# Two row sums of a graph network's last node pass as adding DMAs instead of VectorE additions

## The reference

```python
h = jnp.maximum(_layernorm(x, axis=-1), 0.0)
x = x + _L0_gnn_ref(h, ..., src, dst)               # conv with attention, batch norm over all nodes
h = jnp.maximum(_layernorm(x, axis=-1), 0.0)
x = x + _L1_gnn_ref(h, edge_attr_32, edge_index_t, ...)

# inside _L1_gnn_ref
pairs = jnp.concatenate([node_vectors, boxes], axis=1)
c = _gelu(pairs @ W_c1 + b_c1)
combined = _gelu(c @ W_c2 + b_c2)
return node_vectors + combined
```

## Time and profile before

| what | value |
|---|---|
| median of 3 runs | 2105.99 us (2104.59 to 2109.98) |
| span of the profiled execution, first to last instruction | 1817.9 us |
| median of the runs less that span | 288.1 us |
| busy over the span: PE, PEld, DVE, ACT, POOL | 80%, 54%, 82%, 47%, 62% |
| mean granted TensorE clock | 0.851 of full speed |
| share of the 16 DMA engines: SP's queue, POOL's queue | 41.1%, 7.4% |
| DVE's first addition of the second node pass (L879) | at 743.2 us |
| its last row sum (L891) | at 1282.5 us |

### The profile page before, as it was taken

How to read it: one execution, slowest core, us unless ns; L and a number is a source line. 1 busy time by engine, 2 the same in 40 slices (tenths; PEclk the granted TensorE clock), 3 DMA queues, 4 the chain that set the end, 5 groups by cost and what they waited for, 6 DMA issues and landing times.

```text
span 1817.9 us, 22722 instructions
## 1 busy us (share of the span) xinstructions
PE 1463.3 (80%) x6619; PEld 980.4 (54%) x6619; DVE 1485.5 (82%) x2772; ACT 849.3 (47%) x1497; POOL 1129.4 (62%) x989
## 2 busy tenths in 40 slices
PE   3465556488888888588988988889599999999993
PEld 2133233367777777366656666666345555555541
DVE  8799999688988887798899789888268788788781
ACT  4477777322233222365666566665123433434341
POOL 7777788777777777787500000868756776434446
PEclk9788897667777777797899689888789999999996
DMA  7467664777754333344444434555344453343410
GB/s 232 156 219 229 210 212 157 245 249 261 269 200 130 120 108 110 120 169 159 153 151 165 143 142 163 179 181 174 115 114 146 129 150 106 112 129 101 123 52 17
DMA packets 139616, 286.41 MB, mean 158 GB/s; under 512 B 31154, under 2 KB 48379, under 8 KB 139496
## 3 DMA queue, kind: packets, MB, share of 16 engines
q1 hardware_dynamic: 107176, 254.36, 41.1%
q0 software_dynamic: 32320, 30.62, 7.4%
HBM read 164.51 MB, written 121.80 MB: 157 GB/s over the span
## 4 chain that ended last, share of the span: by engine, by line
PE 48%; DVE 29%; issue 11%; POOL 4%; ACT 4%; DMA 3%; SPq 0%; DVEq 0%; POOLq 0%; ACTq 0%
PE banks L1400 7%; DVE stat L697 5%; PE banks L1390 5%; PE banks L1454 4%; DVE stat L705 4%; PE banks L1321 3%; PE banks L1477 3%; PE banks L1475 3%; PE banks L1484 2%; DVE sums L780 2%; PE banks L1304 2%; DVE xc L711 2%; PE banks L1448 2%; POOL agg_ring L577 2%; PE banks L1372 2%
## 5 line engine op out<-in xcount | busy, mean ns | idle before, releaser
L577 POOL DMA_INDIRECT agg_ring<-agg_rows,edge_idx x196 | 234.6, 1197 | 331.4 <-DMA edge_agg<-agg_ring 270.1
L581 POOL DMA_INDIRECT out<-agg,put_last x196 | 207.6, 1059 | 167.1 <-DVE agg L976 109.9
L577 POOL DMA_INDIRECT x_ring<-in_x,edge_idx x200 | 239.8, 1199 | 63.3 <-issue 60.9
L581 POOL DMA_INDIRECT agg_rows<-agg,put_first x196 | 229.2, 1169 | 59.7 <-issue 57.9
L577 POOL DMA_INDIRECT gout<-in_x,edge_idx x192 | 217.1, 1130 | 58.5 <-issue 57.3
L1400 PEld LDWEIGHTS banks<-packed,cT 96*128 96x128 f32 (+1 forms) x1568 | 202.4, 207 | 43.3 <-issue 42.0
L1400 PE MATMUL banks<-packed,cT 96*128 96x64 f32 (+1 forms) x1568 | 208.8, 291 | 0.0
L1265 PE MATMUL banks<-ident,xc 128*128 128x128 f32 (+1 forms) x784 | 131.4, 316 | 94.1 <-DVE xc L711 94.1
L1265 PEld LDWEIGHTS banks<-ident,xc 128*128 128x128 f32 (+1 forms) x784 | 110.5, 165 | 147.1 <-DVE xc L711 107.7
L1274 PE MATMUL banks<-hT,packed 128*128 128x512 f32 (+1 forms) x196 | 126.8, 781 | 76.3 <-ACT hT L1031 76.3
L1390 PE MATMUL banks<-hT,packed 64*96 64x512 f32 (+1 forms) x392 | 128.5, 735 | 46.4 <-ACT cT L1131 40.8
(11 more groups left out here) (153 smaller groups left out, 3135.9 us busy)
## 6 DMA issues: line engine op xcount, KB each, us to landing
xt<-in_x SPq DMA_DIRECT2D x96, 512.0 KB, 4.2
r_rows<-rT SPq DMA_DIRECT2D x48, 512.0 KB, 5.9
xe<-edge_x SPq DMA_DIRECT2D x96, 256.0 KB, 4.6
agg_rows<-rb SPq DMA_DIRECT2D x48, 512.0 KB
rT<-r_rows SPq DMA_DIRECT2D x48, 512.0 KB, 5.6
out<-xt SPq DMA_DIRECT2D x48, 512.0 KB, 2.6
edge_r<-rr SPq DMA_DIRECT2D x48, 256.0 KB, 3.9
rr<-edge_r SPq DMA_DIRECT2D x48, 256.0 KB, 4.8
```

The source lines that it names most:

```text
L577: A.indirect_dma_start(to, None, table[:, :], bass.IndirectOffsetOnAxis(ap=idx, axis=0), bounds_check=limit, oob_is_err=False).then_inc(si ...
L581: A.indirect_dma_start(table[:, :], bass.IndirectOffsetOnAxis(ap=idx, axis=0), rows_of, None, bounds_check=limit, oob_is_err=False).then_i ...
```

## The change

The two DVE additions `add_h2` and `final_rows` of the second node pass become DMAs from SBUF to SBUF with an adding write, issued by POOL. Semaphores that counted DVE instructions become sets of DMA semaphores (`B_y` one of 3, `B_fin` one of 6). POOL's program is merged: `put_agg` of the first 36 groups (`PUTS_AHEAD`), then 51 turns, one for each step s: `add_h2(s)`, `add_out(s - 2)` and one group of agg's DMAs, `put_agg` of the groups 36 to 48 in turns 0 to 12 and `gather_agg(s - 13)` from turn 13 on; then the other 11 groups of `gather_agg`. SP stashes up to `a - 14` groups instead of `3 * (i - 16)`. The semaphores of the x loads of the second pass are those of the first pass, counted on.

```diff
+PUTS_AHEAD = 36
+FIN_LAG = 2
...
-    def __init__(self, sems, incs=16):
-        self.sems, self.incs = sems, incs
+    def __init__(self, sems, incs=16, first=0):
+        self.sems, self.incs, self.first = sems, incs, first
...
-        B_x = slots("rows_loaded", XS)
+        B_x = Slots(A_x.sems, first=S)
-        B_y = stage("x2_plus_h2")
+        B_y = slots("h2_added_to_x2", CS)
-        B_fin = stage("final_row_ready")
+        B_fin = slots("out_gelu_added", XS)
...
             def store_final(s):
-                sp.wait_ge(B_fin.sem, B_fin.after(s))
+                sp.wait_ge(B_fin.of(s), B_fin.after(s))
...
-                due = min(G, max(stashed, 3 * (i - 16)))
+                due = min(G, max(stashed, a - 1 - G + PUTS_AHEAD))
...
+            def add_h2(s):
+                p = nodes_of(s)
+                pool.wait_ge(B_h.sem, B_h.after(s))
+                A.dma_start(xt[s % XS][0:p, :], xc[s % CS][0:p, :], accum_op=ALU.add).then_inc(B_y.of(s), 16)
+
+            def add_out(s):
+                p = nodes_of(s)
+                pool.wait_ge(B_og.sem, B_og.after(s))
+                pool.wait_ge(B_y.of(s), B_y.after(s))
+                A.dma_start(xt[s % XS][0:p, :], gout[s % 2][0:p, :], accum_op=ALU.add).then_inc(B_fin.of(s), 16)
...
-            for n in range(G):
+            for n in range(PUTS_AHEAD):
                 put_agg(n)
-            G_p.all_done(pool, G)
-            for g in range(G):
+            for s in range(S + FIN_LAG):
+                if is_step(s):
+                    add_h2(s)
+                if is_step(s - FIN_LAG):
+                    add_out(s - FIN_LAG)
+                n = PUTS_AHEAD + s
+                if is_group(n):
+                    put_agg(n)
+                if n == G:
+                    G_p.all_done(pool, G)
+                if is_group(n - G):
+                    gather_agg(n - G)
+            for g in range(S + FIN_LAG + PUTS_AHEAD - G, G):
                 gather_agg(g)
...
-            def final_rows(s):
-            def add_h2(s):
...
-            for i in range(PAIRS + 1):
+            for i in range(PAIRS):
...
-                if is_step(a - 2):
-                    final_rows(a - 2)
...
-                if a in pair:
-                    add_h2(a)
-                if is_step(a - 1):
-                    final_rows(a - 1)
-                if b in pair:
-                    add_h2(b)
```

More of the change, by code:

```diff
@@ L55 @@
 class Slots:
-    def __init__(self, sems, incs=16):
-        self.sems, self.incs = sems, incs
+    def __init__(self, sems, incs=16, first=0):
+        self.sems, self.incs, self.first = sems, incs, first
     def of(self, step):
-        return self.sems[step % len(self.sems)]
+        return self.sems[(self.first + step) % len(self.sems)]
     def after(self, step):
-        return (step // len(self.sems) + 1) * self.incs
+        return ((self.first + step) // len(self.sems) + 1) * self.incs
     def done(self, eng, step):
@@ L506, in load_prev @@
                     sp.wait_ge(B_t.sem, B_t.after(S - 1))
-                    sp.wait_ge(B_y.sem, B_y.after(S - 1))
+                    B_y.all_done(sp, S)
                 load_same(mask[g % MS], prev_row, g, g, 0, P, C_sm)
```

## The result

The changed kernel took 2220.1 us (median of 4 runs, 2207.0 to 2227.1), the kernel before beside it 2108.0: +112 us. The ratio on record is 1.0633, 95% interval 1.0535 to 1.0731; that of the two medians is 1.053, and why the two differ is open. Forecast were +56 us and 2162; the sign and the range (2100 to 2245) held, the size was off by a factor of two.

The account below looks back on a forecast made before the run. PE's round, not DVE, was taken to bound the second pass. Pairs +49, start +18 and end -11 gave +56 on 2106, so 2162 us (range 2100 to 2245); 288 us outside the profiled span were taken as they are.

Parts of the forecast that it names:

- The old loop, -0.3 us a pair: Second node pass: removing four DVE additions a pair saves only 0.3 us, giving 20.3 us at full clock.
- d = 1.5: POOL's time to issue one SBUF-to-SBUF adding DMA, in us; high end 2.3, low end 1.27.
- c = 5.5: POOL's time for a group of four scatters, in us, range 5.1 to 5.9.
- L = 5.5: Time from issue to landing of an adding DMA, in us, range 3.4 to 9.
- POOL's work in a pair is then 17 us of about 21: Second pass: two groups and four adding DMAs fit a pair, so POOL's load sets no bound, only its order.
- R + 0.1: Start of POOL's add_h2(a), 0.1 us for the semaphore after R, the end of relu_scale(a).
- R + 15.6: Landing of the sum of a-1 after relu_scale(a) ends (R); before the change it was ready at R + 3.5.
- r chain: Late sum delays SP's store, r load, norm_r and h2 copy: 23.7 us a pair, +49 us in 22 pairs.
- Start, +18: Pass start: POOL reaches turn 0 at 783 after 36 groups, so DVE's L707 of step 3 waits; +18 us.
- End, -11: End of pass: earlier stashes let the masks issue 13 us earlier, less 2 for three stashes; -11 us.
- Rival 1: DMA engines fill up, every landing grows: 27.4 us a pair, 2255 to 2278 us; chance 0.17.
- rival 2: All adds are hidden, the sum of a-1 landing by R + 9.7: 0 us, 2106; chance 0.13.

Follow-up runs that it names:

- e11: Changed kernel with h2's sum back on DVE, only out's sum as DMA, stashes first, r loads earlier, 28 puts ahead: 0.978 of the kernel before (1788 us), again 0.963.
- e7: Changed kernel with stashes first, r loads behind a pair's first store, both DMAs as plain copies without adding: 2053 us, 0.984 of the kernel before.
- e2: Changed kernel with SP's stashes at the head of an iteration, ahead of its stores: 1941 us, 1.057 of the kernel before.
- e10: Changed kernel, unchanged, run again beside the kernel before, without pauses: 2008 us, ratio 1.097.
- e9: Kernel before, unchanged, run again without pauses: 1829 us, ratio 1.000.
- set 2: Runs e5 to e8, with pauses, beside the kernel before, which took 2100.9 us there.
- e6: Changed kernel with stashes first, r loads behind a pair's first store, 28 puts ahead instead of 36: 2098 us, 1.009 of the kernel before.
- e5: Changed kernel, unchanged, run again with pauses: 2216 us, 1.068 of the kernel before.
- e8: Kernel before, sums on DVE, with only the changed kernel's earlier stash formula (a - 14): 2044 us, 0.978 of the kernel before.
- set 5: Runs with pauses: e11 again (2061 us) and its orders with both sums on DVE (2089 us), beside the kernel before at 2145.8 us.
- e16: e6's kernel run again, without pauses: 1875 us, 1.024 of the kernel before.

## Why the prediction was right in sign and wrong in size

- **The old loop, -0.3 us a pair: held in size.** Four DVE additions of a pair were worth next to nothing. At a granted clock of 0.92 a pair takes 20.6 us in the kernel before, 20.5 in e11 with two of them gone and 20.6 to 20.7 in e7, where the last sums are left out; at 1.00 it is 19.5 before, 19.0 to 19.5 in e11 and 19.0 in e7 (the first two pairs left out).
- **POOL's prices.** "d = 1.5" each was 0.60 + 1.30 and 0.30 to the next for two, 2.2 and not 3.0; "c = 5.5" was 5.0 to 5.9. These held well enough. "L = 5.5" was 5.0 for h2's sum and 8.3 for out's: mis-sized, since the second DMA of a turn stands behind the first, and both count twice on the engines. The high end of 9 took it in.
- **"POOL's work in a pair is then 17 us of about 21: not a bound of its own. Its order is."** This is the step that failed. I followed POOL's order as issues only, and let `add_h2(a)` start at R + 0.1. The group between two sums is a `gather_agg`, which waits for a buffer of the ring; the stash that frees it stood in SP's queue behind `store_final(a-1)`, and so behind POOL's own last sum. R + 0.1 was R + 10.7. With the landing's excess the sum of a-1 came at R + 27.6 and not R + 15.6. Put into the forecast's own formula, (27.6 - 15.6)/2 = 6.0 more a pair, this makes 23.7 into 29.7 us; measured are 30.2. As the 27.6 is itself read in pairs of 30.2, that only shows that the r chain was right and was fed late; what sets the time is the circle, 29.6 us by its own landings, and what shows it is e2. In e10's pass the pairs behind the first two cost 151 us, where the forecast had 49.
- **Where the circle doesn't act**, the forecast's pair of 23.7 is too low by 1 to 3 us: 25.0 early in e10, 25.5 and 26.6 in e2, with r still behind a sum that lands 3 us later than I took.
- **Start, +18: about right without pauses.** e10's POOL comes to turn 0 at 784.73, forecast 783:

```profile
784.73 1.05 POOL L615 DMA_DIRECT2D xt<-xc  x1
```

```profile
789.66 1.22 DVE L729 TENSOR_REDUCE stat<-xt 128x16 f32<-128x1024 f32 x1 [13.89 <-DMA xt<-xc]
```

  The first two pairs cost 12.7 us more than e9's. In the kernel after's own run the term is absent: POOL waits 122.3 us for DVE instead, having scattered on through the pause.
- **End, -11: failed.** It was +17.7 (e10 against e9). "SP has 36 groups stashed by then" and so no wait: but the circle runs on behind the pass, POOL's last gathers are late, and SP stands 18.4 us in five stashes ahead of the masks. DVE waits for these 30.9 us (30.2 in e10), where the kernel before waited 19.5. The first loads of the last stage, behind the late store of the pass, cost some 6 us more. SP and DVE of the kernel after, whose last L903 is at 1633.34:

```profile
1685.87 18.41 SPq L516 DMA_DIRECT2D edge_agg<-agg_ring  x5
1704.46 1.80 SPq L428 DMA_DIRECT2D rb<-prev_row  x4
```

```profile
1656.54 0.69 DVE L934 TENSOR_TENSOR rr<-rr,bn 128x512 f32<-128x512 f32 x1 [10.94 <-DMA weighted<-edge_agg]
...
1708.35 1.27 DVE L945 TENSOR_TENSOR_SCAN sums<-rb,sums,banks 64x512 f32<-64x512 f32 x1 [30.92 <-issue]
```

  With the stashes first (e2) that last wait is 10.0 us, and the rest is 555 us, 6 under e9's.
- **The base.** "Taken as they are" hid some 270 us inside the runs' spans (2108 against 1834). The forecast's span was 1874 us, 1953 with its high ends, and e10's is 2007: without pauses the range would have failed, and that 2220 lies in it is luck. The cost of the change is some 30 to 60 us smaller with pauses than without. Three things would make it so: in set 2 the pass begins at 921 us with 28 puts ahead (e6), at 955 to 960 with 36 (e5, e7) and at 978 with all 49 (e8), though in set 5 it begins at 964 and 997 with 28; there is no start term (13 to 18 us); and the old pass may be slower there. Their sum is argued, not shown, and what the engines stand still for stays open: no run touched it.
- **The rivals.** Rival 1, full DMA engines, is not what happened, but it is part of what stood next: a share of 0.86 with the orders mended. Rivals 2 and 3 fell (rival 2's 0.8 us for L is 0.7 by its own terms). Rival 3's mechanism, DVE as the limit of the loop, has at most the 0.5 us for it by which pairs at full clock are shorter (19.0 for 19.5): the version that is faster, e11, is so in the main by fewer long pairs, its steady ones taking 20.5 us.

## What to carry to other kernels

When a step moves to another engine's queue, follow every instruction between its neighbours there to what *that* one waits for, and look whether the wait leads back to the moved step: a round through two queues and a small ring costs the sum of its landings, whatever the engines' busy shares say. A free engine is no free resource: two adding DMAs a step took the DMA engines from a share of 0.47 to 0.86 and pairs at a high clock from 20.6 to some 23.8 us; one took them to 0.78 and left the pairs at 20.5. Check that the profiled span and the timed runs are of one kind before building a sum on the first.

## What the runs showed of the hardware

- An adding DMA of 512 KB from SBUF to SBUF takes all 16 DMA engines 2.76 us (2.90 by e10), a copy 1.41; they land in 5.0 and 3.2 us, and a second add 0.6 us behind the first in 8.3.
- One kernel on one chip took 1828 us in one set and 2101 in another, the surplus being stretches in which PE, DVE and ACT stand still while POOL's scatters go on, with "remote" as the profile's only releaser.
- With the same matmuls, a pass that keeps an even 20.5 us a pair was granted a clock of 0.91, one whose pairs swing from 19.5 to 24.7 us one of 0.85 (both between the levels of 1.2 and 2.4 GHz). Which is cause and which effect no run here separates, and the first kernel run again was granted 0.86.
- At a granted clock of 0.71 a pair takes 24.7 us with PE busy 22.66, whether both sums are DMAs (e16) or DVE's (before).
